# Matrix exponentials in a fused attention and expert-mixture kernel: how the squarings are counted, when the scale is applied, and in which order the stage's work is issued

## The reference, cut to what matters

```python
xn = layernorm(x) * ln_gamma + ln_beta
abel_out = gelu(xn @ abel_w + abel_b)
topw, topi = top_k(xn @ moe_gate_w + moe_gate_b, 2)        # 2 of 8 experts
h = gelu(einsum('bsd,edh->ebsh', xn, ew1) + eb1)           # ew1 (8, 256, 512)
eo = einsum('ebsh,ehd->ebsd', h, ew2) + eb2
moe_out = einsum('ebsd,bse->bsd', eo, w_dense)
for i in range(3):
    moe_out = moe_out @ expm(gens[i])                      # gens (3, 256, 256)
```

## Time and profile before

| | |
|---|---|
| median of the timed runs | 1361.19 us (1360.8 to 1362.25) |
| profiled execution: span | 1360.3 us |
| busy over the span | PE 86%, weight loads 75%, DVE 63%, ACT 36%, POOL 30% |
| chain that ended last | PE 60%, issue 7%, DVE 6%, DMA 4% |
| stage of `weights()` | 0 to 126 us of the span |

### The profile page before, as it was taken

One profiled execution on the slowest core, in us unless ns is written; L12 is line 12 of the kernel. 1 busy time (PEld: TensorE's weight loads), 2 busy tenths in 40 slices (PEclk: granted clock), 3 DMA queues, 4 the chain that ended last, 5 costly groups with the idle time before them and its releaser, 6 DMA issues.

```text
span 1360.3 us, 26013 instructions
## 1 busy us (share of the span) xinstructions
PE 1172.3 (86%) x7280; PEld 1018.5 (75%) x7281; DVE 861.9 (63%) x2756; ACT 495.3 (36%) x967; POOL 412.5 (30%) x480
## 2 busy tenths in 40 slices
PE   6796878986899999973699989999992999999958
PEld 5673656874788889962589877888881888989947
DVE  6536677876566666655876668767546566666646
ACT  1010553442434444431233333334451444444435
POOL 3001111577344444430000000104555344444410
PEclk9898997787999999996899999998996999999989
DMA  8500123354444533324011011001237443533357
GB/s 284 169 0 8 63 89 114 132 199 160 148 136 132 180 108 89 89 84 178 0 48 47 2 47 47 1 1 59 100 123 232 159 119 114 166 108 101 112 184 252
DMA packets 72271, 149.15 MB, mean 110 GB/s; under 512 B 10918, under 2 KB 36210, under 8 KB 72186
## 3 DMA queue, kind: packets, MB, share of 16 engines
q1 hardware_dynamic: 51626, 92.87, 19.8%
q0 software_dynamic: 19776, 54.45, 13.1%
q10 hardware_dynamic: 784, 0.79, 0.2%
HBM read 82.63 MB, written 65.44 MB: 109 GB/s over the span
## 4 chain that ended last, share of the span: by engine, by line
PE 60%; issue 7%; DVE 6%; DMA 4%; POOL 2%; ACT 2%; SPq 1%; POOLq 1%; DVEq 0%; ACTq 0%
PE bank L2150 17%; PE bank L1694 8%; PE bank L1695 8%; PE bank L1696 7%; PE bank L1564 6%; PE bank L1720 4%; PE bank L1773 2%; PE bank L1703 2%; PE bank L2208 2%; DMA xh<-slots_in 2%; PE bank L188 1%; POOL xh L1356 1%; DVE work L1933 1%; DVE xs L1920 1%; PE bank L2161 1%
## 5 line engine op out<-in xcount | busy, mean ns | idle before, releaser
L1694 PE MATMUL bank<-ew,rows 128*128 x852 | 298.0, 350 | 4.5 <-DVE rows L1230 2.4
L1695 PE MATMUL bank<-low_in,rows 128*128 x852 | 273.6, 321 | 0.0
L1696 PE MATMUL bank<-ew,rows 128*128 x852 | 272.3, 320 | 0.0
L1367 POOL DMA_INDIRECT results<-xh x142 | 141.8, 998 | 293.1 <-DVE xh L1258 274.0
L1694 PEld LDWEIGHTS bank<-ew,rows 128*128 128x128 f32 x852 | 161.6, 190 | 15.4 <-issue 8.0
L1696 PEld LDWEIGHTS bank<-ew,rows 128*128 128x128 f32 x852 | 161.1, 189 | 11.5
L1695 PEld LDWEIGHTS bank<-low_in,rows 128*128 128x128 f32 x852 | 162.0, 190 | 6.0
L1531 ACT ACTIVATE xh<-bank 128x512 f32<-128x512 f32 x142 | 85.0, 598 | 217.7 <-PE bank L1696 217.7
L1267 DVE TENSOR_TENSOR rows<-bank,rows 128x512 fp32r<-128x512 f32 x142 | 98.2, 691 | 95.0 <-ACT rows L200 95.0
L1346 POOL DMA_INDIRECT slots_in<-xh,work x120 | 118.0, 983 | 81.4 <-DVE work L1127 47.7
L636 POOL TENSOR_TENSOR work<-work,mhalf 128x8 f32<-128x8 f32 (+1 forms) x22 | 38.7, 1760 | 316.7 <-DVE work L629 316.6
(11 more groups left out here) (334 smaller groups left out, 2031.7 us busy)
## 6 DMA issues: line engine op xcount, KB each, us to landing
xh<-slots_in POOLq DMA_DIRECT2D x142, 129.0 KB
low_in<-low SPq DMA_DIRECT2D x32, 512.0 KB
xh<-results SPq DMA_DIRECT2D x14, 1032.0 KB, 5.5
dense<-ab SPq DMA_DIRECT2D x12, 512.0 KB, 4.8
xs<-in_L_attn_a_x_dram SPq DMA_DIRECT2D x4, 1024.0 KB
ew<-in_L_ffn_ew_dram SPq DMA_DIRECT2D x2, 2048.0 KB, 14.3
ew<-in_L_ffn_ew_dram SPq DMA_DIRECT2D x4, 1024.0 KB, 13.6
low<-xh SPq DMA_DIRECT2D x8, 512.0 KB, 2.7
```

The costliest lines, as they stand in the source:

```text
L1367: pool.indirect_dma_start(out=yg, out_offset=bass.IndirectOffsetOnAxis(ap=back[j % RING], axis=0), in_=yr[j % RING], in_offset=None).then_ ...
L1694: pe.matmul(o, hi, f32r(high(c)), start=(c == 0), stop=False)
L1695: pe.matmul(o, hi, f32r(low(c)), start=False, stop=False)
L1696: last = pe.matmul(o, lo, f32r(high(c)), start=False, stop=(stop and c == chunks[-1]))
```

## The change

- The count: beside the greatest absolute row sum of A (now compared with 8 x 2^k), the greatest absolute row sum of A² is compared with 4^k; both are counted per partition, the larger count is taken, and the greatest of the partitions' counts, at least 1, is s. So TensorE's transpose and spread now carry a count, and come behind A³.
- A is no longer scaled. PE waits for the generators only, and transposes, squares and cubes them as they are. 2^-s, 4^-s and 8^-s go into a table of 12 factors (`factor`), that each polynomial term and each Horner sum reads as an operand of one value per partition, where constants stood before. GpSimd writes the 12 fixed parts of the table, one memset each.
- VectorE makes the terms of a Horner round just before the sums of that round, and the bias parts come after the rounds.
- TensorE puts centrings 0, 1 and 2 between the steps of the rotation product, VectorE accordingly.

The diff, cut to its core (the renamed buffers and semaphores are left out; `centre(e)` on each engine is the old body of its centring loop):

```diff
-A = a.take(NROT, KC, C)
+A2_at = a.take(NROT, KC, C)
...
-polys = [A, a2.take(NROT, KC, C), a2.take(NROT, KC, C), X]
+polys = [gens, a2.take(NROT, KC, C), a2.take(NROT, KC, C), X]
 A3 = a3.take(NROT, KC, C)
-A2 = gens
-ratio = [1.0 / ((3 * i + 1) * (3 * i + 2) * (3 * i + 3)) for i in range(POLY)]
+A, A2 = gens, A2_at
+shares_of = [[1.0 / (3 * i + 1) for i in range(POLY)],
+             [1.0 / ((3 * i + 1) * (3 * i + 2)) for i in range(POLY)],
+             [1.0 / ((3 * i + 1) * (3 * i + 2) * (3 * i + 3)) for i in range(POLY)]]
+fixed = a2.take(3, POLY)
+factor = a2.take(3, POLY)
...
+        for k in range(3):
+            for i in range(POLY):
+                pool.memset(fixed[:, k, i:i + 1], shares_of[k][i]).then_inc(factors_ok, 1)
         pool.memset(onesf[:], 1.0).then_inc(consts, 1)
...
+        then(v.tensor_tensor(thr_square, thr, thr, ALU.mult))
+        then(v.tensor_scalar(thr_norm, thr, 8.0, None, ALU.mult))
         v.wait_ge(w_gens, 16)
-        then(v.tensor_reduce(gsum, gens.rearrange("p m c j -> p (m c) j"), AX.X, ALU.add,
-                             apply_absolute_value=True))
-        v.tensor_reduce(gmx, gsum, AX.X, ALU.max).then_inc(g_mx, 1)
+        then(v.tensor_reduce(gsum, A.rearrange("p m c j -> p (m c) j"), AX.X, ALU.add, apply_absolute_value=True))
+        then(v.tensor_reduce(norm, gsum, AX.X, ALU.max))
+        then(v.tensor_scalar(over, thr_norm, norm, None, ALU.is_lt))
+        for m in range(NROT):
+            v.wait_ge(A2_ps, m + 1)
+            v.tensor_copy(A2[:, m], bank[:, NROT + m, :].rearrange("p (c j) -> p c j", c=KC)).then_inc(A2_ok, 1)
+            v.wait_ge(A2_ok, m + 1)
+            then(v.tensor_reduce(ssum[:, m * KC:(m + 1) * KC], A2[:, m], AX.X, ALU.add, apply_absolute_value=True))
+        then(v.tensor_reduce(square, ssum, AX.X, ALU.max))
+        then(v.tensor_scalar(over_square, thr_square, square, None, ALU.is_lt))
+        then(v.tensor_tensor(over, over, over_square, ALU.max))
+        v.tensor_reduce(gmx, over, AX.X, ALU.add).then_inc(g_mx, 1)
         v.wait_ge(g_row, 1)
         v.tensor_reduce(gtop, bank[0:1, 7, 0:P], AX.X, ALU.max).then_inc(g_top, 1)
         v.wait_ge(g_all, 1)
         then(v.tensor_copy(gall, bank[:, 7, P:P + 1]))
-        then(v.tensor_scalar(cmp, thr, gall, None, ALU.is_lt))
-        then(v.tensor_reduce(sf, cmp, AX.X, ALU.add))
-        then(v.tensor_scalar(sf, sf, 1.0, None, ALU.max))
+        then(v.tensor_scalar(sf, gall, 1.0, None, ALU.max))
         v.tensor_copy(sqi, sf).then_inc(s_ok, 1)
         then(v.tensor_scalar(scf, sf, -1.0, 127.0, ALU.mult, ALU.add))
-        then(v.tensor_copy(scale.bitcast(I32), scf))
-        then(v.tensor_scalar(scale.bitcast(I32), scale.bitcast(I32), 23, None, ALU.logical_shift_left))
-        for m in range(NROT):
-            v.tensor_scalar(A[:, m], gens[:, m], scale, None, ALU.mult).then_inc(A_ok, 1)
-        v.wait_ge(A_ok, NROT)
+        then(v.tensor_copy(power[:, 0:1].bitcast(I32), scf))
+        then(v.tensor_scalar(power[:, 0:1].bitcast(I32), power[:, 0:1].bitcast(I32), 23, None, ALU.logical_shift_left))
+        then(v.tensor_tensor(power[:, 1:2], power[:, 0:1], power[:, 0:1], ALU.mult))
+        then(v.tensor_tensor(power[:, 2:3], power[:, 1:2], power[:, 0:1], ALU.mult))
+        v.wait_ge(factors_ok, 3 * POLY)
+        then(v.tensor_tensor(factor, fixed, cols(power, POLY), ALU.mult))
         v.wait_ge(consts, 3)
-        for m in range(NROT):
-            v.wait_ge(A2_ps, m + 1)
-            v.tensor_copy(A2[:, m], bank[:, NROT + m, :].rearrange("p (c j) -> p c j", c=KC)).then_inc(A2_ok, 1)
-        v.wait_ge(A2_ok, NROT)
-        for q, i in enumerate((3, 2, 1, 0)):
+        def poly(q, i):
             for m in range(NROT):
-                v.scalar_tensor_tensor(polys[i][:, m], A[:, m], 1.0 / (3 * i + 1), eye, ALU.mult, ALU.add).then_inc(poly_ok, 1)
+                v.scalar_tensor_tensor(polys[i][:, m], A[:, m], factor[:, 0, i:i + 1], eye, ALU.mult, ALU.add).then_inc(poly_ok, 1)
             for m in range(NROT):
                 v.wait_ge(poly_ok, NROT * q + m + 1)
-                last = v.scalar_tensor_tensor(polys[i][:, m], A2[:, m], 1.0 / ((3 * i + 1) * (3 * i + 2)), polys[i][:, m],
-                                              ALU.mult, ALU.add)
-                last.then_inc(X_ok if i == 3 else b_ok, 1)
+                last = v.scalar_tensor_tensor(polys[i][:, m], A2[:, m], factor[:, 1, i:i + 1], polys[i][:, m], ALU.mult, ALU.add)
+                last.then_inc(X_ok if i == POLY - 1 else b_ok, 1)
+        poly(0, POLY - 1)
+        for q, i in enumerate((2, 1, 0)):
+            poly(q + 1, i)
+            v.wait_ge(b_ok, NROT * (q + 1))
+            for m in range(NROT):
+                v.wait_ge(horner_ps, NROT * q + m + 1)
+                v.scalar_tensor_tensor(X[:, m], bank[:, m, :].rearrange("p (c j) -> p c j", c=KC), factor[:, 2, i:i + 1],
+                                       polys[i][:, m], ALU.mult, ALU.add).then_inc(X_ok, 1)
         v.wait_ge(w_small, 16 * 14)
...
-        for q, i in enumerate((2, 1, 0)):
-            v.wait_ge(b_ok, NROT * (q + 1))
-            for m in range(NROT):
-                v.wait_ge(horner_ps, NROT * q + m + 1)
-                v.scalar_tensor_tensor(X[:, m], bank[:, m, :].rearrange("p (c j) -> p c j", c=KC), ratio[i],
-                                       polys[i][:, m], ALU.mult, ALU.add).then_inc(X_ok, 1)
         v.wait_ge(s_ok, 1)
...
-        v.wait_ge(rot_Y, 1)
-        v.tensor_copy(X[:, 0], bank[:, 6, :].rearrange("p (c j) -> p c j", c=KC)).then_inc(rot_ok, 1)
-        v.wait_ge(rot_Y, 2)
-        v.tensor_copy(R, bank[:, 7, :].rearrange("p (c j) -> p c j", c=KC)).then_inc(rot_ok, 1)
-        for e in range(E):
+        def centre(e):
             v.wait_ge(ew1_ps, e + 1)
             for c in range(KC):
                 v.scalar_tensor_tensor(ew1[:, c, e, :], ew1[:, c, e, :], gam[:, c:c + 1], bank[:, 3 + e % 2, :],
                                        ALU.mult, ALU.add).then_inc(ew1_ok, 1)
+        centre(0)
+        v.wait_ge(rot_Y, 1)
+        v.tensor_copy(X[:, 0], bank[:, 6, :].rearrange("p (c j) -> p c j", c=KC)).then_inc(rot_ok, 1)
+        centre(1)
+        centre(2)
+        v.wait_ge(rot_Y, 2)
+        v.tensor_copy(R, bank[:, 7, :].rearrange("p (c j) -> p c j", c=KC)).then_inc(rot_ok, 1)
+        for e in range(3, E):
+            centre(e)
         v.wait_ge(abw_ps, 1)
...
+        def centre(e):
+            if e >= 2:
+                pe.wait_ge(ew1_ok, KC * (e - 1))
+            for c in range(KC):
+                pe.matmul(bank[:, 3 + e % 2, :], driftb[:, c, :], ew1[:, c, e, :], start=(c == 0), stop=False)
+            pe.matmul(bank[:, 3 + e % 2, :], sel[:, e, :], eb1p[:], start=False, stop=True).then_inc(ew1_ps, 1)
         pe.wait_ge(consts, 2)
-        pe.wait_ge(g_mx, 1)
-        pe.transpose(bank[0:1, 7, 0:P], gmx, ident[:]).then_inc(g_row, 1)
-        pe.wait_ge(g_top, 1)
-        pe.matmul(bank[:, 7, P:P + 1], onesf[:], gtop, start=True, stop=True).then_inc(g_all, 1)
+        pe.wait_ge(w_gens, 16)
         for m in range(NROT):
-            pe.wait_ge(A_ok, m + 1)
...
+        pe.wait_ge(g_mx, 1)
+        pe.transpose(bank[0:1, 7, 0:P], gmx, ident[:]).then_inc(g_row, 1)
         for m in range(NROT):
+            if m == 1:
+                pe.wait_ge(g_top, 1)
+                pe.matmul(bank[:, 7, P:P + 1], onesf[:], gtop, start=True, stop=True).then_inc(g_all, 1)
             pe.wait_ge(A3_ok, m + 1)
...
         transposed(0, X[:, 0], 0).then_inc(rot_T, 1)
-        pe.wait_ge(rot_TS, 1)
-        product(6, AT[:, 0], X[:, 1]).then_inc(rot_Y, 1)
-        pe.wait_ge(rot_ok, 1)
-        transposed(0, X[:, 0], 0).then_inc(rot_T, 1)
-        pe.wait_ge(rot_TS, 2)
-        product(7, AT[:, 0], X[:, 2]).then_inc(rot_Y, 1)
         pe.wait_ge(w_small, 16 * 14)
         pe.wait_ge(w_ew, 16 * (KC + HC))
         pe.wait_ge(drift_ok, KC)
         pe.wait_ge(rows_ok, 1)
-        for e in range(E):
-            if e >= 2:
-                pe.wait_ge(ew1_ok, KC * (e - 1))
-            for c in range(KC):
-                pe.matmul(bank[:, 3 + e % 2, :], driftb[:, c, :], ew1[:, c, e, :], start=(c == 0), stop=False)
-            pe.matmul(bank[:, 3 + e % 2, :], sel[:, e, :], eb1p[:], start=False, stop=True).then_inc(ew1_ps, 1)
+        centre(0)
+        pe.wait_ge(rot_TS, 1)
+        product(6, AT[:, 0], X[:, 1]).then_inc(rot_Y, 1)
+        centre(1)
+        pe.wait_ge(rot_ok, 1)
+        transposed(0, X[:, 0], 0).then_inc(rot_T, 1)
+        centre(2)
+        pe.wait_ge(rot_TS, 2)
+        product(7, AT[:, 0], X[:, 2]).then_inc(rot_Y, 1)
+        for e in range(3, E):
+            centre(e)
         pe.wait_ge(rot_ok, 2)
```

More of the change, by code:

```diff
@@ L235, in weights @@
             p2 = a2.take(H, rows=E, dt=BF16)
-            gsum = a2.take(NROT * KC)
+            STEPS = 24
+            gsum, ssum = a2.take(NROT * KC), a2.take(NROT * KC)
+            norm, square = a2.take(1), a2.take(1)
```

(10 more changed lines are left out.)

## The result

The changed kernel takes 1343.89 us (median of 4 runs, 1340.14 to 1344.42), the kernel before 1360.99 beside it. That is 17.1 us less where 25.5 were forecast; the median lies 1.9 us above the stated range, and the quotient of the two medians is 0.9874. The ratio on record is another one: 0.9845, 95% interval 0.9819 to 0.9871, which stands for some 21 us. 1343.89 is 0.9845 of 1364.98, the median of 16 runs of the kernel before in the next measurement; which runs the ratio was taken against is not on record. By that ratio a kernel before of 1361.19 would come down to 1340.1, inside the range. So the gain in the launch is 17 to 21 us, and no closer. The profiled execution took 1343.67 us with a span of 1341.9, so 1.8 lie around the span.

The account below looks back on a forecast made before the run. It took the weights stage's chain, ending at a barrier, as the bound. Squarings -13.25, earlier start and rounds -11.6, bias parts +2.1, rotations and centrings -2.7: -25.5 us off 1361.19 gives 1335.7, range 1331 to 1342.

Parts of the forecast that it names:

- The interleave: Rotations and centrings: centrings 0, 1 and 2 fill the handovers between rotation steps, so TensorE runs through; -2.7 us.
- The operand price: Horner terms and sums: reading a one-value-per-partition operand instead of a constant costs 0.06 us per VectorE instruction.
- all but 0.4 us: If the clock falls in the 3.5 us hole before round one, VectorE's terms hide the delay except 0.4 us.
- The clock: Step on TensorE's clock around the 3.5 us hole before round one: sum -25.1 by the skill's rule, otherwise -25.5 us.
- What moved behind the rounds: Bias parts between the last Horner sum and the loop delay the second squaring's transposes; +2.1 us.
- The barrier passes the gain on one to one: Stage's end: the span gains what the stage gains; a later stage over 2 us longer or shorter would refute it.
- 1: Rival: the clock does not recover after the hole before round one; up to 14 us over three rounds, 6 in 100.
- 2: Rival: the squaring loop runs more than three times; four 1342.3, five 1348.9 us; 2 in 100.
- 3: Rival: the loads of ew1 and ew2 last past 67 and set the end; 1338 to 1345 us, 2 in 100.
- 4: Rival: the stage never reaches the higher clock; +60 us, 1396; 3 in 100, 1 more for a milder form.
- 5: Rival: more gain, by zero operand price, closer packing or better clock phase later; 1326 to 1331 us, 4 in 100.
- The row of 36 to 37: Old profile's clock row: after TensorE's last product near 32.8 the clock fell within 36 to 37, after some 4 us.

Follow-up runs that it names:

- g1: Changed kernel with 7 idle matmuls on TensorE in the 3.5 us hole before Horner round one; ratio 0.9829 to the kernel before.
- g3: Changed kernel with 7 idle matmuls in the hole before round one and abb's bias parts moved behind the squaring loop; 1365.3 us, ratio 0.9784 to the kernel before.
- the first six: Profiles of the kernel before, the changed kernel and the first four follow-up kernels; time after the stage's end 1234.1 to 1240.7 us.
- e3: Changed kernel with the rotation product and then all eight centrings one after the other again; ratio 0.9884 to the kernel before.
- e4: Changed kernel with constants in place of the one-value-per-partition operands in the 24 terms and 9 sums; 1342.2 us, ratio 0.9852 to the kernel before.
- g0: Changed kernel run a third time with no edit, beside later follow-ups; 1379.0 us, ratio 0.9869 to the kernel before.
- f0: Changed kernel run again with no edit, beside later follow-ups; ratio 0.9884 to the kernel before.
- e2: Changed kernel with the first comparison against 2^k instead of 8 x 2^k, so five squarings run; 1357.8 us, ratio 0.9951 to the kernel before.

## Why the prediction was right or wrong

- Direction, places and the largest terms held. Three squarings and not five: 13.2 us, measured 13.5. The interleave: 2.7, measured 2.9. The operand price of 0.06: 2.0 us over the rounds, as forecast. The norms of A² under TensorE's products, the count behind them, the factors at 23.1: measured 23.3. That start was in part luck: it was 22.2 to 23.9 in other profiles of the same early text. The loads were no bound: the DMA share is 0 from 56 on, and the first centring starts at 71.8.
- Too small was "all but 0.4 us" under **The clock**. I let the clock return 3.3 us after the restart, as it had at 47, and hid the rest under VectorE's terms. It was down from 25.2 to 32, 5.8 us beyond the restart, and round one's last sum started at 34.5, 1.8 us late. In seven profiles with this hole the rounds were 0.4 to 1.9 us longer than the 22.3 of g1 and g3, where the hole is filled.
- Left out was a part of **What moved behind the rounds**. The pause of 2.2 us was forecast as 2.1, but priced as a delay only. The 0.64 us that the loop's start takes on VectorE, now bare, was not in it, nor the clock's fall behind it, 1.3 to 1.7 us in six of eight profiles. I had looked for such a fall in the 3.5 us hole alone. The two pauses together make 1.8 + 0.5 + 1.4 = 3.7 of the 4.0 that the stage missed; the rest is the factors' 0.2 and the last digits.
- "The barrier passes the gain on one to one" failed its own test, 3.1 us against the 2 that I had allowed, but the test was too weak to decide: it takes one profile of each kernel, and the rests of the first six differ by 6.6 us, more than the few us that I added to the range. Of the 8.4 us between the 25.5 forecast and the 17.1 of the medians, 4.0 are the stage's, 3.1 lie behind it in the two profiles with no cause shown, and 1.3 between the profiles' spans and the medians. By the recorded ratio, some 21 us, the stage's 4.0 are nearly all.
- None of the rivals came. 1: the clock returned in every profile. 2: nine loop copies, three squarings. 3: the loads ended before 56. 4: the squarings ran at 6.6 us or at most 8.6. 5: the operand price was there. The Trainium skill's rule on an idle TensorE ("TensorE: Matmul & The Clock Gate", section "What's actually happening") decided rightly between the two outcomes weighed, and the sum itself went by the other: the clock fell inside the hole in six of the seven profiles where it was 3.5 us long, and 1.3 us behind it in e3. It did not fall in e4, where the hole was 3.26 us. The row of 36 to 37, on which I had set the sum, showed one case of when.

## What to carry to other kernels

Price a new pause of TensorE twice, once as a delay and once as the stretch at the lower clock behind it, also where it is as short as 2 us; moving small vector work out of one idle place can open another. Idle matmuls of just the right length, and moving the vector work once more to where nobody waits, together gave back 5.5 us of the stage (g3 against g0, from the first term on), and idle matmuls of twice the length gave back nothing. Where later stages have pauses of their own, compare the stage's end as well as the span, over several profiles.

## What was not expected of the hardware

The clock fell after idle stretches of very different length: 1.7 us after the last matmul in f0 (PEclk 0.81 in 23 to 24), 2.5 us in the changed kernel, 4 us in the kernel before. It also fell where TensorE had already begun again, behind a pause of 2.2 us (PEclk 0.94 in 55 to 56, 0.50 in 56 to 57) and in e3 behind the hole. In the same program the pause of 2.2 us was followed by a squaring of 8.2 to 8.3 us three times, and with little else changed (e2, e4) by one of 6.9. An fp32 matmul of 256 columns at the higher clock shows as two records of 0.22 us each, so `product` is two output blocks of two accumulating matmuls, four matmuls and eight records, and not the four blocks that the kernel's description above gives it.
